# Weighing the keys in flamingo attention with the keys stationary and the probabilities moving, sums and reciprocals by DMA

## The reference, cut to what matters

```python
def _L0_xattn_ref(q, kv, Wq, Wk, Wv, Wo, bo):      # q 32x128x128, kv 32x128x64
    qh = (q @ Wq).reshape(B, N, 16, 64).transpose(0, 2, 1, 3)
    kh = (kv @ Wk).reshape(B, M, 16, 64).transpose(0, 2, 1, 3)
    vh = (kv @ Wv).reshape(B, M, 16, 64).transpose(0, 2, 1, 3)
    scores = jnp.einsum('bhnd,bhmd->bhnm', qh, kh) * scale
    attn = jax.nn.softmax(scores, axis=-1)
    out = jnp.einsum('bhnm,bhmd->bhnd', attn, vh)
    return out.transpose(0, 2, 1, 3).reshape(B, N, INNER) @ Wo + bo

def _L0_ffn_ref(hidden_states, ...):               # 4096 tokens of 128, 32 experts
    topk_idx, topk_w = _gate(x, gate_w, gate_bias)
    g = jnp.einsum('th,eih->eti', x, expert_gate)
    u = jnp.einsum('th,eih->eti', x, expert_up)
    outs = jnp.einsum('eti,ehi->eth', jax.nn.silu(g) * u, expert_down)
    ...
x = x + jnp.tanh(g_xattn[0]) * _L0_xattn_ref(_layernorm(x), ctx_512, ...)
x = x + jnp.tanh(g_ffn[0]) * _L0_ffn_ref(_layernorm(x), ...)
```

## Time and profile before

| | us |
|---|---|
| median of 3 runs | 705.96 |
| lowest and highest | 703.84, 706.68 |
| the profiled execution | 703.62 |
| its span, first to last instruction | 701.8 |
| TensorE, VectorE, ScalarE, Pool busy | 683.8, 512.6, 331.3, 266.2 |
| mean granted TensorE clock, share of full | 0.995 |

### The profile page before, as it was taken

One profiled execution on the slowest core, in us unless ns is written; L12 is line 12 of the kernel. 1 busy time (PEld: TensorE's weight loads), 2 busy tenths in 40 slices (PEclk: granted clock), 3 DMA queues, 4 the chain that ended last, 5 costly groups with the idle time before them and its releaser, 6 DMA issues.

```text
span 701.8 us, 15942 instructions
## 1 busy us (share of the span) xinstructions
PE 683.8 (97%) x4700; PEld 580.8 (83%) x4700; DVE 512.6 (73%) x1640; ACT 331.3 (47%) x627; POOL 266.2 (38%) x316
## 2 busy tenths in 40 slices
PE   8799999999999999999999898999999999999997
PEld 6589889888889889889998686878787888878785
DVE  6775877768767777687567596877778686969565
ACT  3243344434443344434344555555555555555553
POOL 4212121222122121212310264656666565756654
PEclk9999999999999999999999999999999999999999
DMA  5401000000000000000000554535363636455550
GB/s 134 131 19 27 17 19 18 22 18 18 18 18 18 19 17 18 24 18 18 18 2 1 115 131 95 136 90 138 86 160 79 165 91 155 106 124 136 111 148 15
DMA packets 44815, 47.27 MB, mean 67 GB/s; under 512 B 11744, under 2 KB 27232, under 8 KB 44768
## 3 DMA queue, kind: packets, MB, share of 16 engines
q1 hardware_dynamic: 44768, 46.72, 27.4%
HBM read 43.81 MB, written 2.62 MB: 66 GB/s over the span
## 4 chain that ended last, share of the span: by engine, by line
PE 89%; POOL 4%; issue 4%; DVE 1%; DMA 1%; ACT 0%; POOLq 0%; SPq 0%; DVEq 0%
PE bank L1105 16%; PE bank L1029 13%; PE bank L1031 13%; PE bank L1030 13%; PE bank L1137 8%; PE bank L1065 5%; PE bank L1113 5%; POOL halves L457 4%; PE bank L1085 3%; PE bank L1091 2%; PE bank L1088 2%; PE bank L1094 2%; PE bank L1152 1%; PE bank L1036 1%; PE bank L1075 1%
## 5 line engine op out<-in xcount | busy, mean ns | idle before, releaser
L457 POOL TENSOR_TENSOR halves<-area,halves 128x512 fp32r<-128x512 f32 x135 | 174.6, 1293 | 145.0 <-ACT halves L580 139.4
L537 ACT ACTIVATE area<-bank 128x512 f32<-128x512 f32 x128 | 69.5, 595 | 190.7 <-PE bank L1094 190.7
L593 ACT ACTIVATE area<-bank 128x512 f32<-128x512 f32 x136 | 81.3, 597 | 112.6 <-PE bank L1031 111.8
L989 DVE TENSOR_TENSOR bank<-area,bank 128x512 f32<-128x512 f32 x128 | 88.6, 692 | 55.4 <-PE bank L1031 54.7
L1105 PE MATMUL bank<-ctx_keys,area 128*128 128x65 f32 x1024 | 123.1, 271 | 0.0
L1105 PEld LDWEIGHTS bank<-ctx_keys,area 128*128 128x128 f32 x1024 | 120.6, 192 | 0.4 <-issue 0.4
L1029 PE MATMUL bank<-x2t_hi,w_hi 128*128 128x512 f32 x272 | 110.4, 406 | 2.2 <-DVE area L997 2.1
L1031 PE MATMUL bank<-x2t_lo,w_hi 128*128 128x512 f32 x272 | 107.0, 393 | 0.0
L710 DVE TENSOR_REDUCE row_max<-bank 128x4 f32<-128x512 f32 x128 | 82.0, 684 | 33.5 <-PE bank L1065 28.9
L1030 PE MATMUL bank<-x2t_hi,w_lo 128*128 128x512 f32 x272 | 106.5, 392 | 0.0
L405 POOL TENSOR_TENSOR ctx_hi<-ctx_raw,ones_col 128x128 fp32r<-128x128 f32 x32 | 12.8, 400 | 238.7 <-PE bank L1094 232.2
(11 more groups left out here) (119 smaller groups left out, 1099.0 us busy)
## 6 DMA issues: line engine op xcount, KB each, us to landing
wbc<-rows_dram SPq DMA_DIRECT2D x128, 256.0 KB, 4.4
w_raw<-experts SPq DMA_DIRECT2D x32, 102.0 KB, 2.0
ctx_raw<-ctx_t SPq DMA_DIRECT2D x64, 32.0 KB, 2.1
out<-area SPq DMA_DIRECT2D x7, 256.0 KB, 4.2
ctx_keys<-ctx_nat SPq DMA_DIRECT2D x32, 32.0 KB, 1.8
max_rows<-max_t SPq DMA_DIRECT2D x64, 4.0 KB
area<-wq_t SPq DMA_DIRECT2D x1, 512.0 KB, 4.6
area<-wo SPq DMA_DIRECT2D x1, 512.0 KB, 4.4
```

The lines of the kernel that those rows point to most:

```text
L457: nc.gpsimd.tensor_tensor(hid_lo[:, u % SLOTS, :], hid[:, u % HIDS, :], raw(hid_hi[:, u % SLOTS, :]), ALU.subtract).then_inc(hidlo_ready, 1)
L537: nc.scalar.activation(probs_t[:, k, :, :], st_ps[q][:].rearrange("p (h n) -> p h n", h=4), ACT.Exp)\
L593: nc.scalar.activation(silu_g[:, u % 2, :], gate_ps[u % 2][:], ACT.Silu).then_inc(silu_ready, 1)
L989: nc.vector.tensor_tensor(up_ps[u % UPS][:], silu_g[:, u % 2, :], up_ps[u % UPS][:], ALU.mult)\
```

## The change

`weigh` now takes the keys as the stationary operand and moves the probabilities of four heads at once, 512 columns. u comes out transposed: the key's columns on partitions, the queries along the row. For q = 0 the stationary block is keys and ones (65 columns), so u is on partitions 0 to 63 and the sums on partition 64; for q = 1 it is ones, zeros and keys (128 columns), so the sums are on partition 0 and u on 64 to 127. `ctx_keys` grows for that, and the keys are loaded twice. `transpose_u` and VectorE's `normalise` go.

ScalarE copies each of the four results from PSUM to `u_raw` (`u_out`). SP then spreads the rows of sums to 64 partitions of 16 (`spread_sums`), VectorE takes the reciprocals (`invert`, 128x16), SP writes them to DRAM (`store_inverse`) and reads them back, each row spread over 64 partitions (`spread_inverse`, two DMAs of 256 KB into the one buffer `inverse_bc`), and Pool multiplies (`normalise_batch`, two operations of 64 partitions x 1024). `project_out` runs three batches late instead of two. The last two batches are projected between expert units 4 and 5 and between 10 and 11 of the first chunk (`LATE`), and the last chunk's second layer norm moves into expert chunk 1.

The diff, cut to its core:

```diff
-LN2_AT = {4: range(0, 6), 5: range(6, 9), 6: range(9, LN_LEVELS)}
-SEAM = (1, 7, 11, 15, 18, 21)
+LN2_AT = {6: range(0, 6), 7: range(6, LN_LEVELS)}
+SEAM = (1, 7, 13, 21)
+LATE = {NB - 2: 5, NB - 1: 11}
...
-        u_norm = area[:, 2:4, :].rearrange("p a (h q d) -> p a h q d", h=PAIRS, q=2)
+        u_even = area[:, 2:4, :].rearrange("p q (h n) -> p q h n", h=2)
...
-        ctx_keys = sb("ctx_keys", [P, CB, CD + 1])
+        ctx_keys = sb("ctx_keys", [P, CB, 3 * CD])
+        u_odd = sb("u_odd", [P, 2, 2, CT])
+        u_raw = (u_even, u_odd)
+        sums = sb("sums", [P, 2, HEADS])
+        inverse = sb("inverse", [P, 2, HEADS])
+        inverse_bc = sb("inverse_bc", [P, 2, CT])
...
             def load_keys(b, t):
-                sp.dma_start(ctx_keys[:, b, 0:CD], ctx_nat[:, bass.ds(t, 1), :].rearrange("m a d -> m (a d)"))\
-                    .then_inc(keys_in[b], 16)
+                for q in range(2):
+                    sp.dma_start(ctx_keys[:, b, 2 * q * CD:2 * q * CD + CD],
+                                 ctx_nat[:, bass.ds(t, 1), :].rearrange("m a d -> m (a d)")).then_inc(keys_in[b], 16)
...
+            def spread_sums(t, parity):
+
+                wait_first(u_ready, 4 * t + 4)
+                for q in range(2):
+                    row = CD if q == 0 else 0
+                    sp.dma_start(sums[rows(q), parity, :], u_raw[parity][row:row + 1, q, :, :]).then_inc(sums_in, 16)
+
+            def store_inverse(t, parity):
+
+                wait_first(inverse_ready, t + 1)
+                sp.dma_start(inverse_dram[parity].rearrange("q (p n) -> (q p) n", n=HEADS), inverse[:, parity, :])\
...
+            def spread_inverse(t, parity):
+
+                wait_first(inverse_out, 16 * t + 16)
+                wait_first(norm_ready, 2 * t)
+                for q in range(2):
+                    sp.dma_start(inverse_bc[rows(q), :, :].rearrange("p h n -> p (h n)"),
+                                 inverse_dram[parity, q:q + 1, :].broadcast_to([HD, 2 * CT])).then_inc(inverse_in, 16)
...
+                    if not (first and b == 0):
+                        spread_sums(t - 1, (b - 1) % 2)
+                        store_inverse(t - 1, (b - 1) % 2)
+                        spread_inverse(t - 1, (b - 1) % 2)
...
             sp.sem_inc(result_free, 16)
+            spread_sums(NB - 1, (NB - 1) % 2)
             store_rows(0)
-            for g in range(WBC_SLOTS):
+            load_group(0, 0)
+            store_inverse(NB - 1, (NB - 1) % 2)
+            load_group(0, 1)
+            spread_inverse(NB - 1, (NB - 1) % 2)
+            for g in range(2, WBC_SLOTS):
                 load_group(0, g)
...
+            def normalise(t, parity, q):
+
+                nc.gpsimd.tensor_tensor(u_t[rows(q), parity, :, :].rearrange("p i n -> p (i n)"),
+                                        u_raw[parity][rows(q), q, :, :].rearrange("p h n -> p (h n)"),
+                                        inverse_bc[rows(q), :, :].rearrange("p h n -> p (h n)"), ALU.mult)\
+                    .then_inc(norm_ready, 1)
+                pool.wait_ge(norm_ready, 2 * t + q + 1)
+
+            def normalise_batch(t, parity):
+                pool.wait_ge(inverse_in, 32 * t + 32)
+                wait(pool, attn_done, t - 1)
+                for q in range(2):
+                    normalise(t, parity, q)
 
             def attention(c, first, last):
                 for b in range(CB):
                     t = CB * c + b
+                    if not (first and b < 2):
+                        normalise_batch(t - 2, b % 2)
                     split_weights(b % 2, t, 2 * c + b // 2, NB if last else t + CB)
...
+                    if first and u == 5:
+                        pool.wait_ge(inverse_in, 32 * NB)
+                        pool.wait_ge(attn_done, NB - 2)
+                    if first and u == 7:
+                        pool.wait_ge(hidlo_ready, u + 1)
+                    if first and u in (5, 7):
+                        normalise(NB - 1, (NB - 1) % 2, (u - 5) // 2)
 
             x2t_low(0, 0)
+            normalise_batch(NB - 2, NB % 2)
             in_all_chunks(experts_low)
 
...
 
-            def ut_out(t, parity, r):
-                act.wait_ge(ut_done, 2 * t + r + 1)
-                wait(act, attn_done, t - 1)
-                nc.scalar.activation(u_t[:, parity, 4 * r:4 * r + 4, :],
-                                     ut_ps[:].rearrange("p (h n) -> p h n", h=4), ACT.Copy).then_inc(ut_ready, 1)
+            def u_out(t, parity, h, q):
+
+                act.wait_ge(u_done, 4 * t + 2 * h + q + 1)
+                wait(act, norm_ready, 2 * (t - 1))
+                held = slice(0, CD + 1 if q == 0 else P)
+                nc.scalar.activation(u_raw[parity][held, q, h, :], u_ps[q][held, :], ACT.Copy).then_inc(u_ready, 1)
 
...
                     if not (first and b == 0):
-                        ut_out(t - 1, (b - 1) % 2, 0)
+                        for q in range(2):
+                            u_out(t - 1, (b - 1) % 2, 1, q)
...
                     exp_of(t, 1, 0)
                     exp_of(t, 1, 1)
-                    if not (first and b == 0):
-                        ut_out(t - 1, (b - 1) % 2, 1)
                     if last and b == 2:
                         sigmoid_high(0, scores_ps[1])
                         sigmoid_low(0, scores_ps[1])
+                    u_out(t, b % 2, 0, 0)
                     if b % 2 == 1 and not last:
                         g_high(2 * c + 2 + b // 2, b // 2)
...
-            def normalise(t, parity, h, q):
-
-                k = 2 * h + q
-                u = u_ps[q][:, 0:4 * (CD + 1)].rearrange("p (h d) -> p h d", h=4)
-                dve.wait_ge(u_done, 4 * t + k + 1)
-                wait(dve, inv_ready, 4 * t + k - 3)
-                nc.vector.reciprocal(inv_sum[:, k, :], u[:, :, CD]).then_inc(inv_ready, 1)
-                dve.wait_ge(inv_ready, 4 * t + k + 1)
-                wait(dve, ut_done, 2 * (t - 2) + h + 1)
-                nc.vector.tensor_tensor(u_norm[:, parity, pairs_of(h), q, :], u[:, :, 0:CD],
-                                        inv_sum[:, k, :].unsqueeze(2).broadcast_to([P, 4, CD]), ALU.mult)\
-                    .then_inc(norm_ready, 1)
+            def invert(t, parity):
+
+                dve.wait_ge(sums_in, 32 * t + 32)
+                wait(dve, inverse_out, 16 * (t - 1))
+                nc.vector.reciprocal(inverse[:, parity, :], sums[:, parity, :]).then_inc(inverse_ready, 1)
...
-                            residual(t - 2)
+                        if h == 1 and not (first and b < 3):
+                            residual(t - 3)
                         if not last:
...
                                 ln_apply(c + 1, t - b + CB)
                         if not first:
+                            if step_of_chunk == 6:
+                                dve.wait_ge(x2_ready, t - b)
...
 
-                        for q in range(2):
-                            if h == 1:
...
+                        if h == 1 and b % 2 == 1 and not last:
+                            g_low(2 * c + 2 + b // 2, b // 2)
                         if step_of_chunk == 2 and not last:
                             xt_low(c + 1)
...
+                        if h == 1 and not (first and b == 0):
+                            invert(t - 1, (b - 1) % 2)
...
-            residual(NB - 2)
-            route_chunk_0(SEAM[4], SEAM[5])
+            route_chunk_0(SEAM[2], SEAM[3])
+            residual(NB - 3)
             ln2_apply(1, CB)
-            residual(NB - 1, u_ps[0][:, 0:D])
+            invert(NB - 1, (NB - 1) % 2)
 
 
             def levels_at(c, parity, u, place, first, last):
...
-                if first and place == 1 and u == 1:
+                if first and place == 1:
+                    for t, at in LATE.items():
+                        if u == at:
...
-                if first and place == 1 and 1 <= u <= LN_LEVELS:
+                if c == 1 and place == 1 and 1 <= u <= LN_LEVELS:
...
                 wait(dve, hidlo_ready, free_of(HIDS, c, u))
+                if c == 0 and u == 2:
+                    dve.wait_ge(norm_ready, 2 * NB - 2)
...
-                wait(pe, norm_ready, 4 * t + k - 1)
+                wait(pe, u_ready, 4 * t + k - 1)
                 if k == 0:
-                    pe.wait_ge(keys_in[b], 16 * loads)
-                for i in range(4):
-                    ins = nc.tensor.matmul(u_ps[q][:, i * (CD + 1):(i + 1) * (CD + 1)],
-                                           probs_t[:, k, i, :], ctx_keys[:, b, :], start=True, stop=True)
-                ins.then_inc(u_done, 1)
-
-            def transpose_u(t, parity, r):
-                pe.wait_ge(norm_ready, 4 * t + 2 * r + 2)
-                wait(pe, ut_ready, 2 * t + r)
-                for i in range(4):
-                    ins = nc.tensor.transpose(ut_ps[:, i * P:(i + 1) * P],
```

(37 more changed lines are left out.)

43 lines of the change are left out of this document (18 added, 25 removed).

## The result

The changed kernel takes 934.89 us (median of four runs, 933.92 to 937.36), the kernel before beside it 705.64 (703.84 to 706.68): 1.326 times as long, with an interval of 1.322 to 1.330. The forecast was 952, with a range from 885 to 1015.

What follows compares the result with a forecast made beforehand. TensorE bounds the kernel before; after the change, a latency ring through SP's and Pool's queues does. 28 turns of 20.1 us from 42.5 reach 605.3, then +38, 303.0, 3.7, 0.5 and 1.8 outside the span: 952 us, range 885 to 1015.

Steps and rivals of the forecast that it cites:

- The ring: Attention stage: sums, reciprocal, store, spread, multiplications, split, weights, max rows, keys, next sums; no overlap, one turn a batch, 20.1 us.
- T: Sum of the seven latencies in one attention-stage turn, the shortest possible batch: 20.1 us, bounds 18.4 to 22.4.
- term 4: Spread of the reciprocals from DRAM, two DMAs of 256 KB, until Pool starts: 5.1 us, bounds 4.2 and 5.3.
- Term 7: SP's queue from the split through weights' load, max rows and two keys back to the sums: 3.85 us.
- P(29): Issue of the sums of batch 28, after 28 turns from P(1) at 42.5: predicted at 605.3 us.
- The last part: First weighing of hidden units to the end: 303.0 us as before, late projections 3.7, last two multiplications 0.5.
- Weighing at the same price: TensorE, attention stage: one wide float32 product per weigh costs about 0.9 us, the same as four small ones.
- the transposes' gain: TensorE, attention stage: dropping the transposes saves 0.98 us a batch, about 31 us in 32, worth nothing inside the ring.
- the half-price rival: Pool's multiplications: half the partitions cost half, turn 17.8 us, 888 us in all; chance 8%.
- The clock rival: TensorE's clock stays low after pauses, delaying the reciprocal in every second batch: 34 us more, 986 us; chance 8%.
- The rival of TensorE as bound: Attention stage: with a turn under about 10.5 us TensorE sets the pace, 677 us, faster; chance 3%.
- The signs: Attention-stage trace: TensorE's batches about 20 us apart, busy about half, clock under 1; SP's waits for w_lo near 9 us.

Runs made afterwards that it cites:

- e1: The changed kernel with Pool's split of the weights moved ahead of the two multiplications: 768.51 us, 1.0905 times the kernel before.
- e2: The changed kernel with four slots for the weights' pieces instead of two, Pool's order kept: 770.95 us, 1.0936 times the kernel before.
- e12: e10 with both halves of u in one tile, sum rows copied separately by ScalarE, one 128-partition multiplication a batch, arithmetic complete: 680.15 us, ratio 0.9647.
- e11: e10 with one 128-partition multiplication a batch instead of two, half of the attention's result left out: 676.31 us, ratio 0.9577.
- e6: e1 with ScalarE's g_high ahead of the copies of u and VectorE's reciprocal ahead of g_low: 728.43 us, ratio 1.0352.
- e8: e6 with SP's turn rearranged, keys in one DMA, and four buffers for u instead of two: 713.46 us, ratio 1.0142.
- e9: The kernel before plus two Pool multiplications of 64x1024 a batch on data nobody uses: 728.03 us, ratio 1.0324.
- e10: e8 with VectorE's norm steps moved behind the reciprocal, g_low and routing steps, and a late projection two units later: 703.75 us, ratio 0.9997.
- e4: The changed kernel with three extra float32 products of 512 columns on TensorE at the end of 27 batches: 937.36 us.

## Why the prediction was right, point by point

**The ring and its one turn a batch: right.** e1 and e2 break it at two different places and give 166 and 164 us back.

**Its terms,** from the turn shown above (312.98 to 332.27):

| Term | predicted | measured |
|---|---|---|
| 1 sums' issue to reciprocal | 2.6 | 2.57 |
| 2 reciprocal to the store's issue | 0.5 | 0.34 |
| 3 store's issue to the spread's | 1.75 | 1.63 |
| 4 spread's issue to Pool's start | 5.1 | 4.68 |
| 5 two multiplications | 4.95 | 5.13 |
| 6 split to the weights' load | 1.4 | 1.54 |
| 7 SP's way back | 3.85 | 3.40 |
| T | 20.1 | 19.3 |

The mean of the 28 turns is 19.25. The lower and upper ends that the prediction gave for its terms add up to 18.8 and 21.5, not to 18.4 and 22.4; the measured turn lies in either range.

The two terms that were off most are 4 and 7, by 0.42 and 0.45 us. In term 4 the spread was priced at the one pair of the earlier trace rows, while the earlier trace rows had one such DMA at 4.4 and 3.6; the value stayed within the bounds given, 4.2 and 5.3. Term 7 counted the issue of two keys with gaps as by single rows; they run at 0.82 for both. Both errors have one sign; they make up all of the 0.86 us by which T was too long, since the other five nearly cancel.

**The sum.** The first issue of sums came at 41.46 (42.5 predicted). The one that the prediction called P(29) came at 580.52, where 605.3 stood: 539.1 us for 28 turns in place of 562.8, 23.7 us of the miss. From there to the first weighing of hidden units 40.5 us (38 predicted), so that came at 621.1 instead of 643.3. From that point to the end it took 311.7 us; the prediction had 303.0 + 3.7 + 0.5 = 307.2. Sum: -1.0 - 23.7 + 2.5 + 4.5 = -17.7, which is 932.8 less 950.5. So the parts behind the ring, predicted 7 us too short together, hid a part of the ring's error; that is luck.

**The last part: a term mis-sized.** The prediction took the two multiplications that are left for the experts' stage to be nearly free (0.5) and said 303 to 308. What they cost shows in the first chunk, where TensorE's second late projection waited for Pool:

```profile
641.22 3.75 PE L1185 MATMUL bank<-c_pair,area 128*128 128x128 f32 x16 [2.90 <-POOL area L475]
```

and ran for 3.75 us where one earlier in the kernel took 2.08 (at 318.62). The window from 640 to 646 us, of TensorE alone (its busy time and count, granted clock, DMA share, GB/s), says why:

```profile
640.00:646.00 6.00, 4.78 (x19) 0.50 0.24 66
```

The granted clock is half, 1.2 GHz, behind the pause of 2.90 us; around 318 us it was 0.85. The wait and the longer duration together are 2.90 + 1.67 = 4.6 us, about as much as the last part took beyond the 307.2 predicted. The chunk as a whole (store to store of its rows) took 44.2 us (614.04 to 658.22), 7.4 more than the 36.8 of the kernel before (391.94 to 428.73). The two projections themselves account for 4.0 of it (1.95 and 2.08; 3.7 was predicted), and the wait and the longer duration for 4.6; against that TensorE's other waits in this chunk are some 2 us shorter (4.3 before, 2.2 now). The remainder, under 1 us, stays open, and so does the 1.5 us by which the chunks behind it took longer.

**Weighing at the same price, and the transposes' gain worth nothing: right** for the changed kernel. e12 shows what that gain was, once nothing hides it: 26 us of the 31 that the prediction offered, with a turn 0.7 us shorter than before.

**Pool's price: right** (2.42 predicted at 64x1024, 2.34 measured); the half-price rival fell. **The clock rival:** the clock did fall to 0.80 in the stage, as it said. But the reciprocal came late only in the first turn (4.27 us behind the sums' issue, right behind `g_low`) and 2.47 to 2.62 us behind it in the other 27, so the rival's condition was met once and not in every second batch. **The rival of TensorE as bound,** 677 us if T were under 10.5: not this kernel, but e11 (with half of the result left out) and e12 are that kernel, at 676.3 and 680.2. **The signs:** TensorE's busy share in the stage was to be about half; it is 67% (134.09 of the 200 us from 100 to 300), since at a granted clock of 0.79 its products take longer.

**What the prediction didn't see.** Behind the first ring stood a second, of 26 us for two batches, invisible as long as the first was longer. And Pool's multiplications stretch VectorE's steps. Neither changed this forecast, because the first ring was the longer one; they spoilt the one for e1 (702 expected, 768 measured), where 40 us came back with the second ring (e6), and the one for e8. Had the change been written with the split first, reasoning by the first ring alone would have given "no change" (the 702 us expected of e1) for a kernel that is 9% slower.

## What to carry to other kernels

A wait in an in-order queue costs what stands behind it: before adding a producer to one queue and its consumer to another, follow one turn through all the queues back to its start, add the latencies, and compare the sum with the engines' work per turn; an engine that is 38% busy says nothing here. When a ring is found, look for the next one behind it before pricing its repair, and reorder the cheap instructions ahead of the long waits in every queue it passes. A side engine's long operations aren't free even where nobody waits for them (e9), so lay data out for one operation over all partitions rather than two over half (e12).

## What the runs showed of the hardware

- A Pool multiplication of 1024 float32 columns takes 2.34 us on 64 partitions and 2.35 on 128; in the same way a ScalarE copy of 512 columns takes 588 ns for one partition and 575 for 64.
- A VectorE step of 0.16 us with both inputs in SBUF took up to 2.3 us while such a multiplication ran, and so did one with a single input tile (0.17 us, 2.32 in e10); a step with an input in PSUM didn't change (692 ns). About 4.9 us a batch of Pool work that nobody waits for made the kernel before 3.2% slower (e9).
- From 100 to 300 us the granted clock averaged 0.79 in the kernel after, where TensorE pauses in every turn, and 1.00 in e12, where it is busy 196.99 of 200 us. A rise from 0.80 to 0.86 (e4) was worth nothing where TensorE was off the path.
- The sums' small DMAs from SBUF to SBUF, 64 pieces of 64 bytes each, landed in 1.7 to 3.1 us, 1.9 in the median; the keys' 32 KB from DRAM took 1.8.
